# A transformer layer on one core: operand loads spread over chunks, and transposes and layer-norm statistics moved ahead

## The reference

```python
x = x + attn(layernorm(x))          # q,k,v = xn @ W.T + b
#   scores = (q k^T + q rk[clip(k-q, -20, 20)]) / sqrt(8); a = softmax(scores)
#   out = (a v + a rv[clip(k-q, -20, 20)]) @ Wo.T + bo
x = x + ffn(layernorm(x))           # silu(x wg) * (x wu), then @ wd; int weights / 127
```

## Time and profile before

| | us |
|---|---|
| median of 3 runs | 1430.11 (1429.31 to 1430.37) |
| the profiled execution, its own time | 1427.91 |
| its span, first to last instruction | 1426.0 |
| PE busy | 1281.4 (90%) |
| VectorE busy | 948.1 (66%) |
| ScalarE busy | 758.8 (53%) |
| GpSimd busy | 550.8 (39%) |

### The profile page before, as it was taken

One profiled execution on the slowest core, in us unless ns is written; L12 is line 12 of the kernel. 1 busy time (PEld: TensorE's weight loads), 2 busy tenths in 40 slices (PEclk: granted clock), 3 DMA queues, 4 the chain that ended last, 5 costly groups with the idle time before them and its releaser, 6 DMA issues. The chain is left out here.

```text
span 1426.0 us, 67609 instructions
## 1 busy us (share of the span) xinstructions
PE 1281.4 (90%) x30680; PEld 941.6 (66%) x30688; DVE 948.1 (66%) x1844; ACT 758.8 (53%) x1413; POOL 550.8 (39%) x983
## 2 busy tenths in 40 slices
PE   4377669999999999999999999999999999889998
PEld 2244337777777777777777776777777777656665
DVE  6499777776766766766767667667767676055554
ACT  4276526565655655655656556556556566422222
POOL 4376533543435343435334353434344343022221
PEclk9689859999999999999999999999999999989999
DMA  4445420202020202112020202021120200122321
GB/s 138 114 168 183 155 57 8 53 23 63 9 64 20 53 20 55 25 48 53 20 63 13 64 20 53 21 54 30 43 55 21 64 9 9 41 60 67 89 67 45
DMA packets 101541, 79.08 MB, mean 55 GB/s; under 512 B 13256, under 2 KB 97032, under 8 KB 101256
## 3 DMA queue, kind: packets, MB, share of 16 engines
q1 hardware_dynamic: 101256, 74.77, 19.1%
HBM read 45.90 MB, written 27.26 MB: 51 GB/s over the span
## 5 line engine op out<-in xcount | busy, mean ns | idle before, releaser
L1039 DVE TENSOR_REDUCE b_mx<-b_a 128x1 f32<-128x512 f32 x1024 | 658.7, 685 | 239.2 <-PE b_a L806 233.8
L1000 ACT ACTIVATE b_p<-b_s 128x512 f32<-128x512 f32 x1024 | 569.8, 595 | 417.5 <-PE b_s L847 332.8
L897 PE MATMUL b_pv<-b_p,vg 128*16 128x128 f32 x8192 | 286.8, 275 | 0.0
L770 POOL TENSOR_TENSOR qd<-q,one 48x512 bf16<-48x512 bf16 x256 | 266.1, 1040 | 30.1 <-POOLq L286 5.3
L747 POOL TENSOR_TENSOR b_np<-vg,one 128x16 bf16<-128x16 f32 x192 | 39.1, 264 | 581.1 <-DVE b_mx L1039 570.3
L847 PE MATMUL b_s<-qd,z 112*128 112x32 bf16 (+1 forms) x6016 | 248.9, 189 | 2.8 <-issue 2.8
L806 PE MATMUL b_a<-k,q 48*128 48x512 bf16 x1024 | 203.6, 394 | 28.2 <-DVE b_mx L1039 12.6
L847 PEld LDWEIGHTS b_s<-qd,z 112*128 112x128 bf16 x6016 | 206.0, 99 | 15.2 <-issue 5.3
L897 PEld LDWEIGHTS b_pv<-b_p,vg 128*16 128x16 f32 x8192 | 196.3, 96 | 21.1 <-issue 0.2
L832 PE MATMUL b_s<-q,k 54*128 54x64 bf16 (+3 forms) x4608 | 187.8, 201 | 6.8 <-issue 3.3
L832 PEld LDWEIGHTS b_s<-q,k 54*128 54x128 bf16 (+1 forms) x4608 | 126.2, 95 | 92.2 <-PE b_s L832 29.2
(11 more groups left out here) (125 smaller groups left out, 1312.7 us busy)
## 6 DMA issues: line engine op xcount, KB each, us to landing
x<-in_x SPq DMA_DIRECT2D x32, 256.0 KB, 3.1
scratch_qop<-a_parts SPq DMA_DIRECT2D x16, 384.0 KB, 2.5
scratch_kop<-a_parts SPq DMA_DIRECT2D x16, 384.0 KB, 3.1
k<-scratch_kop SPq DMA_DIRECT2D x32, 192.0 KB
q<-scratch_qop SPq DMA_DIRECT2D x32, 192.0 KB
scratch_v<-a_vr SPq DMA_DIRECT2D x16, 256.0 KB, 3.2
k<-scratch_kop SPq DMA_DIRECT2D x32, 128.0 KB
q<-scratch_qop SPq DMA_DIRECT2D x32, 128.0 KB
```

Source lines behind the costliest of these rows:

```text
L770: nc.gpsimd.tensor_tensor(dst, src, one, ALU.mult).then_inc(s["qd_ready"], 1)
L897: nc.tensor.matmul(PV[32 * a:32 * a + V16, g * P:(g + 1) * P], v[:, 0 if t <= i else 1, t, h, :], PR[at.c % 2][:, t, h, :], start=(t == 0 ...
L1000: nc.scalar.activation(out, src, ACT.Exp, scale=SCALE).then_inc(s["p_ready"], 1)
L1039: nc.vector.tensor_reduce(MX[v.c % 2][:, h:h + 1], PA[(n + hp) % NBANK][:, :], AX_X, ALU.max, negate=True).then_inc(s["a_used"], 1)
```

## The change

Three things are changed, in all three stages.

In the projection stage x, statistics, deviation and normalised rows are made one batch further ahead: step b now makes statistics and deviation of batch b + 3, SP loads x of batch b + 3 at its head, and three batches' statistics and deviations stand before step 0. X of batch 2 is loaded after the tenth `late` load. ACT makes the rows of batch b + 2 before `projected` of batch b + 1, no longer after it.

In the attention stage the twelve operand loads of the next batch are issued one at a time: SP waits for the first bank of chunk c and then issues one piece, pieces 0 to 7 in the eight chunks of the first unit, pieces 8 to 11 in the first four chunks of the second, with the guard rows after the third piece of a unit. The values are loaded in the third unit.

In the output stage PE makes the attention transposes of batch b + 2 between the gates and the downs of batch b, and ACT copies them before it copies the row transposes.

```diff
--- before.py
+++ after.py
@@ -291,14 +291,17 @@
                              d["x"][bass.ds(at.count(), 1)].rearrange("o (t p) e -> p (o t) e", p=P)).then_inc(x_in[at.c % 2], 16)
 
             sp.wait_ge(s["blank"], 1)
-            for dst, src in late:
+            for n, (dst, src) in enumerate(late):
                 sp.dma_start(dst, src).then_inc(s["late"], 16)
+                if n == 9:
+                    sp.wait_ge(s["xn"], 1)
+                    load_x(at0(2))
 
             def step(at):
                 p = at.c % 2
-                if at.plus(2).exists():
-                    sp.wait_ge(s["xn"], at.count(1, 1))
-                    load_x(at.plus(2))
+                if at.plus(3).exists():
+                    sp.wait_ge(s["xn"], at.count(1, 2))
+                    load_x(at.plus(3))
                 v, guard = (d[n][bass.ds(at.count(), 1)].rearrange("o p t -> p (o t)") for n in ("v", "guard"))
                 dsts = [d[n][bass.ds(at.count(), 1)].rearrange("o s p t -> p (o s) t") for n in ("qop", "kop")]
                 for n, ready in ((0, "qsplit"), (1, "ksplit")):
@@ -439,10 +442,10 @@
                     rows(at.plus(1))
                 act.wait_ge(s["kless"], at.count(2, 2))
                 part(at, 1, 2, pk).then_inc(s["ksplit"], 1)
+                if at.plus(2).exists():
+                    normalised(at.plus(2))
                 if at.plus(1).exists():
                     projected(at.plus(1))
-                if at.plus(2).exists():
-                    normalised(at.plus(2))
                 if at.count() == 4:
                     act.wait_ge(s["late"], 16 * len(late))
                     nc.scalar.activation(k["wg"][:, :], wgi[:, :], ACT.Copy, scale=BYTE)
@@ -465,8 +468,8 @@
                 pool.wait_ge(s["rstd"], at.count(1, 1))
                 nc.gpsimd.tensor_tensor(tmp["shift"][:, :], tmp["less"][:, :], tmp["rstd"][:, :], ALU.mult).then_inc(s["shift"], 1)
 
-            deviation(at0(0))
-            deviation(at0(1))
+            for b in range(3):
+                deviation(at0(b))
 
             def step(at):
 
@@ -478,8 +481,8 @@
                 nc.gpsimd.tensor_tensor(PB[p][:, 0, 1, :], QF[p][:, :], PB[p][:, 0, 0, :], ALU.subtract).then_inc(s["pl"], 1)
                 pool.wait_ge(s["pl"], at.count(1, 1))
                 nc.gpsimd.tensor_tensor(PB[p][:, 0, 2, :], qr[:, :], PB[p][:, 0, 1, :], ALU.subtract).then_inc(s["qsplit"], 1)
-                if at.plus(2).exists():
-                    deviation(at.plus(2))
+                if at.plus(3).exists():
+                    deviation(at.plus(3))
                 n = at.count()
                 if n in (1, 2):
                     half = k["q"][1][:, (n - 1) * HH // 2:n * HH // 2, :, :]
@@ -559,7 +562,7 @@
             for tile in (z, rkj, slot):
                 ins = nc.vector.memset(tile[:, :], 0.0)
             ins.then_inc(s["blank"], 1)
-            for b in range(2):
+            for b in range(3):
                 statistics(at0(b))
 
             def step(at):
@@ -580,8 +583,8 @@
                 link(nc.vector.tensor_tensor(db[:, 2, :], dr[:, :], db[:, 1, :], ALU.subtract))
                 nc.vector.tensor_copy(GD[p][:, T * H:], db[:, :, :].rearrange("p c n -> p (c n)"))
                 maxima(1)
-                if at.plus(2).exists():
-                    statistics(at.plus(2))
+                if at.plus(3).exists():
+                    statistics(at.plus(3))
                 maxima(2)
                 maxima(3)
                 dve.wait_ge(s["relmax"], at.count(T, T))
@@ -695,18 +698,21 @@
                 i = at.c % T
                 first = at.plus(-i)
                 ahead = i < LEAD and first.since(T) and first.plus(T).exists()
-                if ahead and i == 0:
-                    sp.wait_ge(s["s_ready"], at.count(NSR))
-                    operands(first, range(0, 3))
-                if ahead and i == 1:
-                    operands(first, range(9, 12))
+                def chunk(c):
+                    sp.wait_ge(s["s_ready"], at.count(NSR, 2 * c + 1))
+
+                if ahead:
+                    for c in range(3):
+                        chunk(c)
+                        operands(first, range(c + SUB * i, c + SUB * i + 1))
                 if at.plus(1).exists():
                     guard_rows(at.plus(1))
-                if ahead and i == 0:
-                    operands(first, range(3, 6))
-                    sp.wait_ge(s["w_ready"], at.count(1))
+                if ahead:
+                    for c in range(3, (SUB, NLOAD - SUB)[i]):
+                        chunk(c)
+                        operands(first, range(c + SUB * i, c + SUB * i + 1))
+                if i == 2 and at.since(T) and at.plus(T).exists():
                     load_values(sp, k, d, at.it * 2 + at.c // T + 1, (at.c // T + 1) % 2)
-                    operands(first, range(6, 9))
                 if at.count() == 4 * T:
                     for p in range(2):
                         sp.wait_ge(xo_out[p], 16 * T)
@@ -1195,12 +1201,12 @@
                     output_projection(after)
                 for c in range(FC):
                     gate_and_up(at, c)
+                if at.plus(2).exists():
+                    attention_transposes(at.plus(2))
                 for c in range(FC):
                     down(at, c)
                 if after.exists():
                     row_transposes(after)
-                if at.plus(2).exists():
-                    attention_transposes(at.plus(2))
 
             run_all(step, 2, B)
 
@@ -1226,10 +1232,10 @@
                     if at.since(1):
                         act.wait_ge(s["hid"], at.count(FC, c - FC + 1))
                     nc.scalar.activation(sg[:, c, :], PG[(at.c * FC + c) % 2][:, :], ACT.Silu).then_inc(s["silu"], 1)
+                if at.plus(2).exists():
+                    transposed_attention(at.plus(2))
                 if at.plus(1).exists():
                     transposed_rows(at.plus(1))
-                if at.plus(2).exists():
-                    transposed_attention(at.plus(2))
 
             run_all(step, 2, B)
```

## The result

The changed kernel takes 1390.42 us (median of 4 runs, 1389.52 to 1391.61) beside 1429.71 us (4 runs, 1427.07 to 1430.37) for the kernel before: a ratio of 0.9729 (0.9712 to 0.9746), or 39 us. The profiled executions have spans of 1387.6 and 1426.0 us, 38.4 apart.

| part of the span | before | after | difference | forecast |
|---|---|---|---|---|
| start to first guard copy | 189.98 | 181.76 | -8.2 | -2 (-7 to +5) |
| first to last guard copy | 1023.05 | 1004.90 | -18.1 | -24 (-30 to -6) |
| last guard copy to the end | 212.97 | 200.94 | -12.0 | -10.2 (-10.5 to -8) |

The account below looks back on a forecast made before the run. PE was taken to bound attention and output, DVE to be busiest in projection. From the profiled 1427.91 us, output -10.2, attention -24 and projection -2 gave 1391.7, or 1394.0 us against the timed median; range 1384 to 1408.

Parts of the forecast that it names:

- The 0.73 us go in the 14 steps: Output stage: PE's idle time before the projection, waiting for ACT's copy of c_aT, disappears; -10.2 us (-10.5 to -8).
- It is in time with 0.2 us left at worst: Output stage: the load of X lands at 1323.3 to 1325.0, before the earlier transposes need it at 1325.2.
- I take four fifths: Attention stage: spreading operand loads wins -24 us of the 30 us excess over undisturbed batches.
- About one per 2 us: Attention stage: the twelve operand loads, one per chunk, go out at about this spacing.
- the K pieces at 392 left PE undisturbed: Attention stage: three K pieces alone filled DMA engines 0.71 for 2 us without a PE gap; basis for -24 us.
- all that SP chains to these steps moves with it: Projection start: operand loads and the stall for x shift with DVE's delay of 1.7 us; +1.7 us (0 to +3).
- go or change their name: Projection, steady part: PE's 20.5 us waiting for normalised rows, while the DVE and POOL loop stays; -2 us (-4.7 to +2).
- The long stall: Projection: DVE's 18.89 us wait for x of batch 4 behind operand loads and values; predicted to remain, for batch 5.
- Gaps stay: Rival, attention stage: spreading does not remove PE's issue gaps, the stage wins only 5 us; 1413 us, chance 0.14.
- The projection gets worse: Rival, projection: POOL splits hold DVE's short operations and early rows delay the Q part; +8 us, 1404 us, chance 0.08.
- Slower: Rival, attention stage: next batch's operands arrive late, over 5.2 us a Q piece, eating the 36 us; chance 0.03.
- More than forecast: Rival, attention and projection: all 30 us of excess won and a projection at -4; 1386 us, chance 0.09.

Follow-up runs that it names:

- the kernel with the spread projection: Changed kernel with batch 0's twelve operand loads issued one per projection step (2 to 13) and its values in step 14: 1373.72 us, ratio 0.9622 to the kernel before.

## Why the prediction was right, and where it was not

The forecast was 1394.0 us and the result 1390.42. The mechanisms of the output and attention stages held, but all three terms were mis-sized: output 1.8 us too small, attention 5.9 too large, projection 6.2 too small. Output and projection came out beyond the bounds that they had been given. That the sum is only some 2 us off is luck: the errors cancel.

- **Output.** "The 0.73 us go in the 14 steps." A step lost 0.94 us. The bracket counts idle time from the end of the row before, but without a pause the next row starts 0.17 us before that end (0.43 us behind the start of a row of 0.60), and the projection reached the gates after 0.90 us instead of 1.00; together 0.27 more than the bracket, of which 0.2 stayed in the step. The term of the sum left that out. 14 x 0.94 = 13.2; 12.0 to 12.5 are in the spans, as the first projection came 0.7 us later behind the last guard copy than before. "It is in time with 0.2 us left at worst" was as thin as it looked: one load of X landed late enough to make a weight load wait, 0.4 us, once.
- **Attention.** The step "I take four fifths" was mis-sized: a batch is 63.85 instead of 63.5, -18.1 to -20.0 us. Of the 30 us over the shortest intervals, spreading took 18.6 (14 x 1.33); 8.9 (14 x 0.63) come with the operand loads even when they are spread, where the prediction had put 6, and the last 2.7 stay without them. "Issue" waits of 6.6 us remained where I had said under 4, though none above 0.8. Two steps behind it failed. "About one per 2 us" does not hold: the guard rows are ready later than the chunk I named, and hold back the pieces behind them, of which three then go out at once. And "the K pieces at 392 left PE undisturbed" was one burst out of fourteen: with Q's loads gone 4.8 us of gaps remain, with K's gone too 0.7. That the gaps come from the burst held, and was shown by copies that have nothing to do with the operands; that they are late instructions is in the traces. That the clock falls behind them held for four of the ten long gaps of the kernel before.
- **Projection, start.** Forecast +1.7 us (0 to +3). The first split was 3.5 us late and not 2.4 (24.24, forecast 23.2), since DVE waited 5.94 us for x of batch 2 and began its statistics at 21.14, 5.6 us after that load was issued, where the prediction had 3.4 to 5.1. Yet the operand loads began at 38.03, before at 38.91. The step that failed is "all that SP chains to these steps moves with it". Before, VectorE's guard division (L588) had started at 37.31 and taken 1.21 us beside POOL's memset, ending with it; now it takes 0.20 (L591) and is through before POOL's memset begins at 37.83. Delay and cover cancelled; by the third step the maxima start 1.4 us earlier than before. That is read from the traces, not tried by itself.
- **Projection, steady part.** -2 forecast, -2.2 measured: the maxima of the third step start at 71.00 before and 69.57 after, those of the thirteenth at 154.86 and 151.26.
- **Projection, last steps.** -1.7 (-3 to 0) forecast, -4.6 measured: the last block of maxima starts at 170.61 before and 162.40 after. The failed step is that PE's 20.5 us of waiting for normalised rows were written off as "go or change their name". In the last steps, without statistics and deviations, VectorE is no longer the one that is always late: before, the transposes waited 1.50 us at 162.75, and the maxima behind them 1.05, 0.76 and 0.30. Putting only the order on ACT back gives 5.7 us back.
- **The long stall** stayed, for x of batch 5 and 17.66 us long, as forecast.
- **The rivals.** "Gaps stay" is out: no gap above 0.84 us in the changed kernel, and the attention part alone is 1.3% faster. Its sign, a gap of over 1 us beside single pieces, did come once, 1.5 us, in the kernel with the spread projection, whose attention stage is the same and whose batches are no slower. "The projection gets worse" is out by its run alone. "Slower" is out: PE waits for no operand at the start of a third unit. Its premise was misread too: "three Q pieces took SP 7.04 us, so one takes 2.3", but a lone one took SyncE 0.69 us (408.94), and the same three, as the first Q pieces of their batch, 2.20 us before (403.93) and 2.27 now. "More than forecast" had all 30 us of the attention stage and a projection at -4; the projection did better than that, at -8.2, and the attention stage did not.

## What to carry to other kernels

Where the busiest engine waits on nothing that a semaphore shows, look at the DMA share just before, and whether the gaps stand at one place of each block of 256 instructions. Where the share is as high as here (0.94 or more for 2 us shortly before every long gap), spread those loads, and check in the queue that they really go out apart, since one wait in their midst bundles them again. A long stall for an input behind a block of loads that are wanted much later is the same case: there it was worth 13 us to send one load per step. And a wait of an engine off the bound is only worth nothing in the stretch from which the bound was read: read the first and the last steps of a loop by themselves.

## What the hardware showed that I had not expected

- Copies from DRAM to DRAM that no engine waits for cost time: 14 bursts of 1.5 MB, 14.6 us in all (14 x 1.04), by gaps on "issue" of up to 1.8 us and once by nearly 7 us at the lower clock behind one of 1.63 us.
- What PE waited for in such gaps was its own next block of 256 instructions: 57 of 57 gaps in three traces end at the same place of the block, 1.2 to 1.8 us after a packet of the instruction queue.
- Removing a wait that the profile shows as 0.73 us shortened the step by 0.94, 1.3 times as much: in a running stream a row starts before the end that is shown for the row in front of it.
- Three Q pieces behind nine other pieces take SyncE 7.50 us, and for most of that time few of the DMA engines are at work. The first three Q pieces of the same batch, at 40.34, took 2.48 us; what holds SyncE the second time no run shows.

```profile
45.17 7.50 SPq L230 DMA_DIRECT2D q<-scratch_qop  x3
```
```profile
49.00:50.00 1.00, 0.00 (x0) 0.00 (x0) 0.00 (x0) 0.00 (x0) 0.00 (x0) 0.50 0.20 72
...
52.00:53.00 1.00, 0.00 (x0) 0.00 (x0) 0.00 (x0) 0.00 (x0) 0.00 (x0) 0.50 0.14 49
```

  The three pieces are copies of 3, 2 and 1 slots from one source, and the slots are their outermost dimension. The Trainium skill, page "DMA: Bandwidth & Descriptors", section "Why a DMA increments its semaphore by 16 and not by 1", has a transfer spread over as many engines, up to 16, as divide the outermost dimension of both its sides. By that rule, as an estimate, 3 and then 2 engines of 16 would be shares of 0.19 and 0.13; the rows, 0.20 and then 0.14, agree, and so do the packets, of which three and then two are under way at a time. It also fits the run without Q's loads: such a piece is long but leaves most engines free.
